# One core, three stages in one launch: the scan recurrence's softplus, shared decays and group norm rearranged, and the attention stage's norms and filter rows moved off VectorE

## The chip, the cores and the metric

The kernel runs on one NeuronCore of a Trainium2 chip. The metric is the device time of one launch in microseconds (us), lower is better. Engines are called by the names that the profile uses: PE is TensorE (matmuls), DVE is VectorE, ACT is ScalarE, POOL is GpSimd, SP is the queue that issues the DMAs.

## The reference, cut to what matters

```python
def reference(x, ...):                       # x: (4, 64, 32, 32); L = 1024 positions, 64 channels
    # 1. two selective-scan blocks (forward, backward) over the 1024 positions
    for d in ("f", "b"):
        xp, z = split(xs @ W_in)             # 128 + 128 channels
        xc = silu(conv2(xp) + conv_b)
        dt_r, Bc, Cc = split(xc @ W_x)       # 8, 16, 16
        dt = softplus(dt_r @ W_dt + b_dt)
        h = exp(dt * A[:, s]) * h + dt * xc * Bc[s]     # 16 states s, 128 channels, in sequence over t
        y = (sum_s h * Cc[s] + D * xc) * silu(z)
        out += y @ W_out
    x = silu(groupnorm(out, 4 groups)) + x
    # 2. causal attention on layer-normed tokens, one head of 64
    t = tokens(x);  t = t + attention(layernorm(t), Wq, Wk, Wv)
    # 3. four "experts" of spectral convolutions (16 filters, prefixes 1, 1/2, 1/4, 1/8 of the sequence)
    t = t + sum_i w_i * stu_i(layernorm(t)[:, :L // 2**i], sigma, phi, M_u[i], M_phi_plus[i], M_phi_minus[i])
    return from_tokens(t)
```

## The kernel before

`build` runs three stages, one after the other, with all engines meeting between them.

**Stage 1, `mamba_stage`.** The work is cut into 8 units: batch entry b (0 to 3) times direction i (forward, backward), u = 2b + i. A unit has 16 states s. For each state DVE makes a drive, `ps_d = ps_x * b_wide` (`drive_step`), and then scans it, `hidden = decay * hidden + drive` (`scan_step`, an instruction over 1024 positions). The decays are exponentials that ACT makes (`decay_of`), the products `prod = hidden * c_wide` are POOL's, and PE adds the 16 products in `ps_y` (`sum_states`). For 4 of the 16 states, `POOL_STATES`, POOL makes the drive into `drive` (`share`) and ACT writes the decay into the PSUM tile `ps_w` (`shared_decay_of`), so that DVE only scans; in the last unit this is so for one state. There are 4 `hidden`, 4 `decay` and `PAIR` = 2 `prod` buffers. While unit u is scanned, the input side of unit v = u + 1 goes through the same `ps_w` on PE and ACT: z, the convolution, the low-rank rows (`take_low`), then dt. dt is a softplus, put together by PE from four parts (`softplus_low`, `softplus_high`) and copied out by `take_dt`; DVE then makes `ps_x = dt * xc` (`dt_x`) and ACT copies it to `dtx` (`keep_dtx`). After the second scan of a unit DVE multiplies the summed `ps_y` of the unit before with its gate (`gate_of`). Each batch entry ends with a product to 64 channels (`out_product`, `norm_take`), a group norm (`norm_stats`, `norm_rstd`, `norm_scale`, `norm_silu`) and a residual sum.

**Stage 2, `attention_stage`.** A prologue and then four slots, slot b for batch entry b. In a slot PE, ACT and DVE go through 12 blocks of transposed scores, exponentials and products for b, and through the scores and row maxima of b + 1 (`reduce`, `maximum`) and the layer norm and projections of b + 2 (`center_x`, `spread_x`, `norm_x`, `normed`, `queries`, `keys`, `values`). DVE also makes the second layer norm of b - 1 (`center_x2`, `norm_x2`). `filter_rows` prepares the filters of stage 3 on DVE in slot 0, after all expert weights have been loaded; POOL weighs and sums the expert matrices (`weigh_and_sum`, `lag_matrices`, `tap_blocks`). The reciprocal roots of all norms are POOL's (`rstd`, `rstd2`).

**Stage 3, `expert_stage`.** PE convolves and mixes 16 filters for two pairs of batch entries. The diff doesn't touch it.

The order on each engine is the order in which its program is written; semaphores (`wait_ge`, `then_inc`) are the only links between engines. Every engine's program for stage 1 is a `batch` function with a loop over s, unrolled for the first and last batch entry and run as a loop for the two between.

## Time and profile before

| what | us |
|---|---|
| three timed runs | 1029.58, 1028.31, 1020.8; median 1028.31 |
| the profiled execution, its own time | 1023.59 |
| its span in the profile | 1021.8 |
| stage 1: start to first scan, scans to the last copy | 37, 508 |
| stage 2 | 161 |
| stage 3 | 315 |
| busy in the span: PE, DVE, ACT, POOL | 859.3, 768.6, 494.0, 539.1 |
| granted TensorE clock, mean, as a share of 2.4 GHz | 0.926 |

The profiled execution lies inside the range of the three runs; 1.8 us of its time lie outside the span. The stage boundaries are read from where the engines start their next program.

### The profile page before, as it was taken

To read this page: it belongs to the slowest core of one execution; us is meant where nothing else is said; L and a number is where in the kernel's file an instruction comes from. 1 tells how busy PE (TensorE), PEld (TensorE's weight loads), DVE (VectorE), ACT (ScalarE), POOL (GpSimd) and SP (SyncE) were. 2 spreads that over 40 slices of the span, in tenths; PEclk is the share of its full clock that TensorE was granted. 3 is DMA by queue.
4 is the path that set the end of the run, shared out by engine and by line. 5 is a ranking of instruction groups with operands and counts; after the bars stand their busy time and mean duration, and the time that the engine had idled before them with its cause. 6 is when DMAs were issued, how large, how long until landed. Compare 5 with 4: busy or idle time off the path is not lost. (4 is left out here: it accounts for less than half of the span.)

```text
span 1021.8 us, 10203 instructions
## 1 busy us (share of the span) xinstructions
PE 859.3 (84%) x3020; PEld 500.5 (49%) x3020; DVE 768.6 (75%) x818; ACT 494.0 (48%) x636; POOL 539.1 (53%) x364
## 2 busy tenths in 40 slices
PE   5669897986878787896676798796999999999996
PEld 2223333332333232332223455444888888888885
DVE  0698999999989999899985668565565656466664
ACT  4355464745646474563302443444455555355554
POOL 3466879786878787875644387332122222122220
PEclk9788999998999999997777989797999999999998
DMA  7667988967879788886517820000233333243332
GB/s 188 220 234 252 335 292 296 323 240 246 299 275 315 242 303 281 275 320 216 207 60 96 94 83 1 0 1 1 83 124 116 105 109 123 83 124 123 123 98 67
DMA packets 74756, 178.20 MB, mean 174 GB/s; under 512 B 23922, under 2 KB 24452, under 8 KB 74708
## 3 DMA queue, kind: packets, MB, share of 16 engines
q1 hardware_dynamic: 74724, 177.82, 54.5%
q8 instruction: 14, 0.23, 0.1%
q14 instruction: 18, 0.15, 0.1%
HBM read 175.54 MB, written 2.26 MB: 174 GB/s over the span
## 5 line engine op out<-in xcount | busy, mean ns | idle before, releaser
L424 POOL TENSOR_TENSOR prod<-hidden,c_wide 128x1024 f32<-128x1024 f32 x128 | 305.8, 2401 | 113.9 <-PE ps_y L512 75.1
L512 PE MATMUL ps_y<-prod,ident 128*128 128x512 f32 x512 | 265.5, 654 | 75.3 <-POOL prod L424 75.1
L815 DVE TENSOR_TENSOR_SCAN hidden<-decay,ps_d 128x1024 f32<-128x1024 f32 x99 | 226.4, 2287 | 13.0 <-DVE ps_d L801 1.9
L1743 PE MATMUL ps_conv<-hankel,u_high 128*128 128x512 f32 (+1 forms) x768 | 215.3, 361 | 0.0
L512 PEld LDWEIGHTS ps_y<-prod,ident 128*128 128x128 f32 x512 | 100.7, 206 | 231.0 <-POOL prod L424 118.1
L1743 PEld LDWEIGHTS ps_conv<-hankel,u_high 128*128 128x128 f32 x768 | 138.6, 189 | 25.6 <-issue 0.3
L1903 DVE TENSOR_TENSOR stack<-ps_conv,stack 64x512 fp32r<-64x512 f32 x128 | 88.3, 690 | 68.8 <-ACT stack L1866 66.4
L1743 PE MATMUL ps_conv<-hankel,u_low 128*128 128x512 f32 (+1 forms) x384 | 138.1, 360 | 0.0
L1626 POOL CAST block_mix<-even 128x256 fp32r (+1 forms) x32 | 12.7, 398 | 218.9 <-PE ps_tail L1725 218.9
L1903 DVE TENSOR_TENSOR qk<-ps_conv,qk 64x512 fp32r<-64x512 f32 x128 | 88.2, 689 | 50.0 <-ACT qk L1866 47.3
L801 DVE TENSOR_TENSOR ps_d<-ps_x,b_wide 128x1024 f32<-128x1024 f32 x99 | 121.3, 1225 | 6.1 <-ACT dtx L680 2.0
L1866 ACT ACTIVATE stack<-ps_conv 64x512 fp32r<-64x512 f32 x128 | 76.1, 594 | 82.3 <-PE ps_conv L1743 80.5
L1866 ACT ACTIVATE qk<-ps_conv 64x512 fp32r<-64x512 f32 x128 | 76.1, 594 | 62.0 <-PE ps_conv L1743 59.9
L686 ACT ACTIVATE decay<-dt_b,a_neg_b 128x1024 f32<-128x1024 f32 x51 | 57.5, 1143 | 51.5 <-DVE hidden L815 51.4
L1743 PEld LDWEIGHTS ps_conv<-hankel,u_low 128*128 128x128 f32 x384 | 72.8, 190 | 13.9
L414 POOL TENSOR_TENSOR drive<-dtx,b_wide 128x1024 f32<-128x1024 f32 x29 | 68.2, 2353 | 13.3 <-ACT dtx L680 13.3
L815 DVE TENSOR_TENSOR_SCAN hidden<-ps_w,drive 128x1024 f32<-128x1024 f32 x29 | 66.1, 2278 | 4.9 <-ACT ps_w L693 4.8
L686 ACT ACTIVATE decay<-dt_f,a_neg_f 128x1024 f32<-128x1024 f32 x48 | 54.1, 1142 | 30.8 <-DVE hidden L815 30.6
L1110 PE MATMUL ps_o<-probs,v_one 128*65 128x512 f32 (+1 forms) x96 | 45.0, 554 | 0.7 <-ACT o_t L1233 0.6
L1358 DVE TENSOR_REDUCE max_parts<-ps_s 128x1 f32<-128x512 f32 (+1 forms) x48 | 27.4, 598 | 16.8 <-PE ps_s L1068 11.9
L1228 ACT ACTIVATE probs<-ps_t 128x512 f32<-128x512 f32 (+1 forms) x48 | 24.9, 523 | 30.4 <-PE ps_o L1110 29.9
L981 POOL TENSOR_TENSOR small<-small,minus_half 128x8 f32<-128x8 f32 x4 | 6.6, 1648 | 49.3 <-DVE small L198 49.3
(293 smaller groups left out, 1179.3 us busy)
## 6 DMA issues: line engine op xcount, KB each, us to landing
b_wide<-bc_rows SPq DMA_DIRECT2D x128, 512.0 KB, 5.0
c_wide<-bc_rows SPq DMA_DIRECT2D x128, 512.0 KB, 4.7
hankel<-filters SPq DMA_DIRECT2D x32, 1026.0 KB, 5.2
plus<-in_M_phi_plus SPq DMA_DIRECT2D x2, 1024.0 KB, 11.1
minus<-in_M_phi_minus SPq DMA_DIRECT2D x2, 1024.0 KB, 16.6
x_pair<-in_x SPq DMA_DIRECT2D x2, 768.0 KB, 8.7
bc_rows<-dt_low SPq DMA_DIRECT2D x8, 128.0 KB, 4.1
out<-plus SPq DMA_DIRECT2D x4, 256.0 KB, 5.0
```

The source lines that it names most:

```text
L414: nc.gpsimd.tensor_tensor(drive[:, :], dtx[:, :], b_wide[s % BC_DEEP][:, :], ALU.mult).then_inc(share_ready, 1)
L424: nc.gpsimd.tensor_tensor(prod[k % PAIR][:, :], hidden[k % DEEP][:, :], c_wide[s % BC_DEEP][:, :], ALU.mult).then_inc(prod_ready, 1)
L512: mm = nc.tensor.matmul(out, ident[:, :], halves(prod[k % PAIR])[h], start=False, stop=(s == N - 1))
L686: nc.scalar.activation(decay[k % DEEP][:, :], dt[i][:, :], ACT.Exp, scale=a_neg[i][:, s:s + 1]).then_inc(decay_ready, 1)
L801: nc.vector.tensor_tensor(ps_d[:, :], ps_x[:, :], b_wide[s % BC_DEEP][:, :], ALU.mult).then_inc(drive_ready, 1)
L815: nc.vector.tensor_tensor_scan(hidden[k % DEEP][:, order], left[:, order], right[:, order], 0.0, ALU.mult, ALU.add).then_inc(hidden_ready, 1)
L1110: nc.tensor.matmul(ps_o[0:C + 1, lo - H * half:], v_one[b % 2][:, kt, :], probs[n % 2][:, 0:hi - lo], start=(kt == 0), stop=True, skip_gro ...
L1228: nc.scalar.activation(probs[n % 2][:, 0:hi - lo], ps_t[n % 2][:, 0:hi - lo], ACT.Exp).then_inc(probs_ready, 1)
L1358: nc.vector.tensor_reduce(max_parts[:, i, at // H:at // H + 1], ps_s[c % 2][:, 0:n], AX.X, ALU.max, negate=True).then_inc(part_ready, 1)
L1743: mm = nc.tensor.matmul(out, pairs[q][wp][:, 2 * delta + source, :], rows, start=(delta == 0 and term == 0), stop=(delta == 2 * half + 1 a ...
L1866: nc.scalar.activation(stacks[slot][0:C, source, b, :, half * 2 * HEAD:(half + 1) * 2 * HEAD], ps_conv[source][lanes(b), half, :, :], ACT. ...
L1903: nc.vector.tensor_tensor(low, ps_conv[source][lanes(b), half, :, :], high.bitcast(F32), ALU.subtract).then_inc(conv_low, 1)
```

## The change

In words, stage 1: the z projection goes ahead in the unit (PE at s = 2 in place of 4), the convolution to s = 3, the low-rank rows to 7, and the waits for the scans of the unit before are gone; the four-part sum is spread over s = 11, 12 and 13, and starts with the rectified part. The shared states are 2, 6, 9 and 15 in place of 2, 5, 9 and 15. The decays of 6 and 9 still go to `ps_w`, and DVE makes the drive of the next state ahead of these scans; those of 2 and 15 go to `ps_d`, the tile of the drives, once the scan before has read it. There are 3 decay buffers for the states that are not shared, and 4 product buffers. `dt_x` reads dt from PSUM. The first unit's softplus is summed by DVE (`first_dt`), and its drive no longer waits for `dtx`. The group norm's sums come from ACT's accumulator (`norm_take`, `norm_squares`) and go through a small DRAM tensor to be spread over the groups. Stage 2: `filter_rows` runs on POOL; `norm_x`, `norm_x2` and the square and rounding of the second norm run on ACT, the latter two norms as 8 ACTIVATEs of 64 columns; the row maximum's rounding is a reduction in place of a cast; four of seven padding memsets went to stage 1; the weights are waited for tensor by tensor.

```diff
-PAIR = 2
+PAIR = 4
+DECAYS = 3
-POOL_STATES = (2, 5, 9, 15)
+POOL_STATES = (2, 6, 9, 15)
+WIDE_SHARED = POOL_STATES[1:3]
...
+def norm_squares(nc, act, g, b, junk, data):
+    act.wait_ge(g.mixed_ready, b + 1)
+    nc.scalar.activation(junk, data, ACT.Square, scale=GN_COUNT ** -0.5,
+                         accum_out=g.sums[:, 1:2]).then_inc(g.squared_ready, 1)
+def store_sums(sp, g, b):
+    sp.wait_ge(g.squared_ready, b + 1)
+    sp.dma_start(g.rows, g.sums[:, :]).then_inc(g.rows_out, 16)
+def load_sums(sp, g, b):
+    sp.wait_ge(g.rows_out, 16 * (b + 1))
+    at_least(sp, g.step, GN_STEPS * b)
+    sp.dma_start(g.group[:, :, :], bass.AP(g.rows.tensor, 0, [[2 * GROUP, C // GROUP], [0, GROUP], [1, 2 * GROUP]])
+                 ).then_inc(g.rows_in, 16)
 def norm_stats(nc, dve, g, b):
-    dve.wait_ge(g.mixed_ready, b + 1)
-    for h in range(2):
-        chain(h + 1, nc.vector.bn_stats(g.bn[:, h, :], g.mixed[:, h * H:(h + 1) * H]))
...
-    chain(10, nc.vector.tensor_scalar(gn[:, 2:3], gn[:, 1:2], group[:, 1:2], GN_EPS, ALU.add, ALU.add))
+    dve.wait_ge(g.rows_in, 16 * (b + 1))
+    chain(1, nc.vector.tensor_reduce(gn[:, 0:2], g.group[:, :, :].rearrange("c k t -> c t k"), AX.X, ALU.add))
+    chain(2, nc.vector.tensor_scalar(gn[:, 2:3], gn[:, 0:1], gn[:, 0:1], -1.0 / GN_COUNT ** 2, ALU.mult, ALU.mult))
+    nc.vector.tensor_scalar(gn[:, 3:4], gn[:, 2:3], gn[:, 1:2], GN_EPS, ALU.add, ALU.add).then_inc(g.step, 1)
...
 # PE, stage 1
                 def gate_in(u, i, b):
-                    scanned(u - 1, POOL_STATES[0])
+                    pe.wait_ge(dtx_ready, u)
                     project(i, b, w_gate[i], z_ready)
...
+                            if s == Y_LAG:
+                                skip_in(u, i)
+                                if ahead:
+                                    conv_in(v, j, bv)
+                            if s == 4 and i == 0 and not first:
+                                pe.wait_ge(xc_ready, v + 1)
+                                out_product(b - 1)
+                            if s == 13 and ahead:
+                                add_logarithm(v, j)
...
-                                if s == 8:
+                                if s == 7:
+                                    scanned(u, WIDE_SHARED[0])
                                     low_rank(v, j)
                                 if s == 10:
-                                    scanned(u, POOL_STATES[2])
+                                    scanned(u, WIDE_SHARED[1])
                                     dt_in(v, j)
+                                if s == 11:
+                                    add_rectified(v)
                                 if s == 12:
-                                    softplus_low(v, j)
-                                if s == 13:
-                                    softplus_high(v, j)
+                                    add_exponential(v)
...
 # ACT, stage 1
                 def shared_decay_of(u, i, s, taken, count):
-                    at_least(act, taken, count)
-                    at_least(act, hidden_ready, u * N + s - 2)
-                    nc.scalar.activation(ps_w[:, :], dt[i][:, :], ACT.Exp,
+                    act.wait_ge(taken, count)
+                    nc.scalar.activation((ps_w if s in WIDE_SHARED else ps_d)[:, :], dt[i][:, :], ACT.Exp,
                                          scale=a_neg[i][:, s:s + 1]).then_inc(share_decay, 1)
...
+                            if s == 2:
+                                shared_decay_of(u, i, POOL_STATES[0], hidden_ready, u * N + POOL_STATES[0])
+                                take_z(v, j, first=first and i == 0)
...
-                            if s == 10:
-                                softplus_exp(v, j)
                             if s == 11:
+                                softplus_exp(v, j, squared=b if i == 0 else 0)
                                 softplus_ln(v, j)
                             if s == 13:
                                 take_dt(v, j)
...
-                            if s == N - 2:
+                            if s == N - 1:
+                                shared_decay_of(u, i, POOL_STATES[3], hidden_ready, u * N + POOL_STATES[3])
                                 keep_dtx(v)
+                nc.scalar.preload_act_table_set("silu_and_others")
...
 # DVE, stage 1
+                def first_dt():
+                    dve.wait_ge(exp_ready, 2)
+                    nc.vector.scalar_tensor_tensor(out=z_raw[:, :], in0=ps_w[:, :], scalar=0.0, in1=soft[:, :],
+                                                   op0=ALU.max, op1=ALU.add).then_inc(sum_step, 1)
+                    dve.wait_ge(one_plus_ready, 1)
+                    dve.wait_ge(sum_step, 1)
+                    nc.vector.scalar_tensor_tensor(out=z_raw[:, :], in0=one_plus[:, :], scalar=-1.0, in1=z_raw[:, :],
+                                                   op0=ALU.add, op1=ALU.subtract).then_inc(sum_step, 1)
+                    dve.wait_ge(ln_ready, 1)
+                    dve.wait_ge(sum_step, 2)
+                    nc.vector.tensor_tensor(dt[0][:, :], dt[0][:, :], z_raw[:, :], ALU.subtract).then_inc(dt_ready, 1)
+                    dve.wait_ge(dt_ready, 1)
+                    nc.vector.tensor_tensor(ps_x[:, :], dt[0][:, :], xc[0][:, :], ALU.mult).then_inc(dtx_ready, 1)
...
                 def dt_x(u, i):
                     dve.wait_ge(dt_ready, u + 1)
-                    at_least(dve, dtx_kept, u)
-                    nc.vector.tensor_tensor(ps_x[:, :], dt[i][:, :], xc[i][:, :], ALU.mult).then_inc(dtx_ready, 1)
+                    dve.wait_ge(dtx_kept, u)
+                    dve.wait_ge(drive_ready, driven_before(u - 1, N - 2) + 1)
+                    nc.vector.tensor_tensor(ps_x[:, :], ps_w[:, :], xc[i][:, :], ALU.mult).then_inc(dtx_ready, 1)
...
+                            if s in shared(final) and s in WIDE_SHARED:
+                                drive_step(u, s + 1, final)
+                            elif s not in shared(final) and not (s - 1 in shared(final) and s - 1 in WIDE_SHARED):
                                 drive_step(u, s, final)
...
 # stage 2: SP, POOL, ACT, DVE
+                store_sums(sp, g, B - 1)
+                load_sums(sp, g, B - 1)
                 load_expert_weights(sp, ins, e)
...
                 rstd(1)
+                filter_rows(nc, pool, e)
                 norm_rstd(nc, pool, g, a.minus_half, B - 1)
...
-                weigh_and_sum(nc, pool, e, 0, 2)
+                weigh_and_sum(nc, pool, e, 0, EXPERTS + 2)
                 rstd(2)
...
+                def norm_x(b):
+                    act.wait_ge(ln_rstd, b)
+                    for i in range(TILES):
+                        last = nc.scalar.activation(xn[:, i, :], cen[:, i, :], ACT.Copy, scale=small[:, 2, i:i + 1])
+                    last.then_inc(xn_ready, 1)
+                def norm_x2(b):
+                    act.wait_ge(ln2_rstd, b + 1)
+                    for i in range(TILES):
+                        last = nc.scalar.activation(u_all[:, i, b, :], cen2[:, i, :], ACT.Copy, scale=small2[:, 2, i:i + 1])
+                    last.then_inc(u_ready, 1)
...
-                    nc.vector.tensor_copy(neg_max[:, tiles, C], low).then_inc(max_high_ready, 1)
+                    nc.vector.tensor_reduce(neg_max[:, tiles, C], max_parts[:, tiles, 0:-(-width(2 * d) // H)], AX.X,
+                                            ALU.min).then_inc(max_high_ready, 1)
...
                         center_x2(b - 1)
-                    else:
-                        filter_rows(nc, dve, e)
```

On DVE, from the gate product of a unit to the state after the second shared scan, in the first batch entry's second unit. Before (`hidden<-ps_w,drive` is a shared scan, here of states 2 and 5; `ps_d<-ps_x,b_wide` is a drive):

```order
L796 TENSOR_TENSOR gated_f<-ps_y,gate_f 128x1024
L815 SCALAR_TENSOR_TENSOR hidden<-ps_w,drive 128x1024
L801 TENSOR_TENSOR ps_d<-ps_x,b_wide 128x1024
L815 SCALAR_TENSOR_TENSOR hidden<-decay,ps_d 128x1024
L801 TENSOR_TENSOR ps_d<-ps_x,b_wide 128x1024
L815 SCALAR_TENSOR_TENSOR hidden<-decay,ps_d 128x1024
L815 SCALAR_TENSOR_TENSOR hidden<-ps_w,drive 128x1024
L801 TENSOR_TENSOR ps_d<-ps_x,b_wide 128x1024
L815 SCALAR_TENSOR_TENSOR hidden<-decay,ps_d 128x1024
```

After:

```order
L863 TENSOR_TENSOR gated_f<-ps_y,gate_f 128x1024
L882 SCALAR_TENSOR_TENSOR hidden<-ps_d,drive 128x1024
L868 TENSOR_TENSOR ps_d<-ps_x,b_wide 128x1024
L882 SCALAR_TENSOR_TENSOR hidden<-decay,ps_d 128x1024
L868 TENSOR_TENSOR ps_d<-ps_x,b_wide 128x1024
L882 SCALAR_TENSOR_TENSOR hidden<-decay,ps_d 128x1024
L868 TENSOR_TENSOR ps_d<-ps_x,b_wide 128x1024
L882 SCALAR_TENSOR_TENSOR hidden<-decay,ps_d 128x1024
L868 TENSOR_TENSOR ps_d<-ps_x,b_wide 128x1024
L882 SCALAR_TENSOR_TENSOR hidden<-ps_w,drive 128x1024
L882 SCALAR_TENSOR_TENSOR hidden<-decay,ps_d 128x1024
```

State 2's scan now reads its decay from `ps_d`, the second shared scan is one state later, and the drive of state 7 stands ahead of it.

On ACT, the end of the same unit: the softplus of the next unit and the last shared decay. Before:

```order
L658 ACTIVATE soft<-ps_w 128x1024
L659 ACTIVATE rectified<-ps_w 128x1024
L661 ACTIVATE soft<-soft 128x1024
L686 ACTIVATE decay<-dt_b,a_neg_b 128x1024
L665 ACTIVATE one_plus<-soft 128x1024
L669 ACTIVATE dt_f<-one_plus 128x1024
L671 ACTIVATE one_plus<-one_plus 128x1024
L686 ACTIVATE decay<-dt_b,a_neg_b 128x1024
L675 ACTIVATE dt_f<-ps_w 128x1024
L693 ACTIVATE ps_w<-dt_b,a_neg_b 128x1024
L686 ACTIVATE decay<-dt_f,a_neg_f 128x1024
L680 ACTIVATE dtx<-ps_x 128x1024
```

After (`late` is the tile that held `one_plus`):

```order
L702 ACTIVATE soft<-ps_w 128x1024
L704 ACTIVATE rectified<-ps_w 128x1024
L706 ACTIVATE soft<-soft 128x1024
L711 ACTIVATE late<-soft 128x1024
L715 ACTIVATE z_raw<-late 128x1024
L718 ACTIVATE dt_f<-late 128x1024
L732 ACTIVATE decay<-dt_b,a_neg_b 128x1024
L722 ACTIVATE dt_f<-ps_w 128x1024
L732 ACTIVATE decay<-dt_f,a_neg_f 128x1024 x2
L738 ACTIVATE ps_d<-dt_b,a_neg_b 128x1024
L727 ACTIVATE dtx<-ps_x 128x1024
```

The last shared decay now stands behind both first decays of the next unit, and goes to `ps_d`.

On ACT, slot 1 of stage 2, around the place of the layer norms (`probs` are the exponentials, `xn` and `u_all` the normed tokens). Before:

```order
L1228 ACTIVATE probs<-ps_t 128x512 x2
L1221 ACTIVATE qk<-ps_m 2x256
L1228 ACTIVATE probs<-ps_t 128x512
L1221 ACTIVATE qk<-ps_m 2x256
L1241 ACTIVATE u_all<-un 128x8x64
L1228 ACTIVATE probs<-ps_t 128x256
L1199 ACTIVATE xn_t<-ps_p 64x512 x2
```

After:

```order
L1324 ACTIVATE probs<-ps_t 128x512 x2
L1317 ACTIVATE qk<-ps_m 2x256
L1276 ACTIVATE xn<-cen,small 128x64 x8
L1324 ACTIVATE probs<-ps_t 128x512
L1317 ACTIVATE qk<-ps_m 2x256
L1324 ACTIVATE probs<-ps_t 128x256
L1286 ACTIVATE u_all<-cen,small 128x64 x8
L1289 ACTIVATE u_high<-u_all 128x8x64
L1295 ACTIVATE xn_t<-ps_p 64x512 x2
L1324 ACTIVATE probs<-ps_t 128x256
```

The two groups of eight and `u_high` are new on ACT and stand between exponentials, in place of one copy.

## Rows read from the trace of the kernel before

**Rows 1.** Busy time by stretch: core, stretch, length, busy of each engine, PEclk, DMA.
```profile
37.00:545.40 508.40, 404.01 (x836) 159.18 (x836) 469.74 (x310) 253.27 (x238) 380.32 (x164) 0.91 0.75 259
545.40:706.50 161.10, 127.21 (x536) 72.46 (x536) 107.64 (x225) 62.10 (x107) 79.75 (x49) 0.87 0.30 44
```

**Rows 2.** Groups of DVE's instructions, by shape, 60 to 525 us: busy, mean, idle before.
```profile
L815 DVE TENSOR_TENSOR_SCAN hidden<-decay,ps_d 128x1024 f32<-128x1024 f32 x94 | 215.0, 2287 | 12.4 <-DVE ps_d L801 1.9
L801 DVE TENSOR_TENSOR ps_d<-ps_x,b_wide 128x1024 f32<-128x1024 f32 x94 | 115.1, 1225 | 4.0 <-DVE gn L151 0.7
L815 DVE TENSOR_TENSOR_SCAN hidden<-ps_w,drive 128x1024 f32<-128x1024 f32 x28 | 63.8, 2279 | 4.9 <-ACT ps_w L693 4.8
L789 DVE TENSOR_TENSOR ps_x<-dt_b,xc_b 128x1024 f32<-128x1024 f32 x4 | 8.2, 2061 | 3.1 <-ACT dt_b L675 3.1
...
L145 DVE TENSOR_SCALAR group_w<-group_t 64x32 f32<-64x32 f32 x3 | 5.5, 1818 | 0.1
L796 DVE TENSOR_TENSOR gated_f<-ps_y,gate_f 128x1024 f32<-128x1024 f32 x4 | 4.9, 1218 | 0.7 <-PE ps_y L512 0.6
```

**Rows 3.** DVE in order of time: the products that end a unit (units 0, 1, 2, 6).
```profile
95.90 1.38 DVE L789 TENSOR_TENSOR ps_x<-dt_b,xc_b 128x1024 f32<-128x1024 f32 x1 [3.09 <-ACT dt_b L675]
...
152.12 1.26 DVE L789 TENSOR_TENSOR ps_x<-dt_f,xc_f 128x1024 f32<-128x1024 f32 x1
...
207.28 3.25 DVE L789 TENSOR_TENSOR ps_x<-dt_b,xc_b 128x1024 f32<-128x1024 f32 x1
...
450.09 1.92 DVE L789 TENSOR_TENSOR ps_x<-dt_b,xc_b 128x1024 f32<-128x1024 f32 x1
```

**Rows 4.** Order of time at the start: first table load, dt's copy, first drive.
```profile
10.63 1.28 ACT L631 ACT_TABLE_LOAD   x1 [10.63 <-PE ps_w L452]
...
31.45 1.02 ACT L675 ACTIVATE dt_f<-ps_w 128x1024 f32<-128x1024 f32 x1 [6.95 <-PE ps_w L486]
...
35.70 1.23 DVE L801 TENSOR_TENSOR ps_d<-ps_x,b_wide 128x1024 f32<-128x1024 f32 x1 [1.96 <-ACT dtx L680]
```

**Rows 5.** DVE in order of time: a group norm's first instruction and the drive behind it.
```profile
223.52 1.38 DVE L135 BATCH_NORM_STATS2 bn<-mixed 64x6 f32<-64x512 f32 x2
...
230.94 1.23 DVE L801 TENSOR_TENSOR ps_d<-ps_x,b_wide 128x1024 f32<-128x1024 f32 x1 [0.19 <-DVE gn L151]
```

**Rows 6.** ACT in order of time: two decays, a copy of 1024 columns, an exponential of 256.
```profile
251.61 2.19 ACT L686 ACTIVATE decay<-dt_b,a_neg_b 128x1024 f32<-128x1024 f32 x2
...
257.56 1.02 ACT L659 ACTIVATE rectified<-ps_w 128x1024 f32<-128x1024 f32 x1
...
573.74 0.39 ACT L1228 ACTIVATE probs<-ps_t 128x256 f32<-128x256 f32 x1 [0.81 <-PE ps_o L1110]
```

**Rows 7.** PE in order of time: sums of 128x1024, at either clock.
```profile
60.87 3.75 PE L452 MATMUL ps_w<-x_pair,w_conv_b 128*128 128x512 f32 x4 [6.12 <-DVE hidden L815]
...
263.11 1.88 PE L486 MATMUL ps_w<-rectified,ident 128*128 128x512 f32 x4
264.82 1.88 PE L512 MATMUL ps_y<-prod,ident 128*128 128x512 f32 x4
```

**Rows 8.** Groups of DVE's instructions, by shape, in stage 2 (527 to 720 us).
```profile
L1372 DVE CAST neg_max<-lowest 128x2 fp32r<-128x2 f32 x8 | 6.7, 834 | 0.3
L1536 DVE TENSOR_TENSOR even<-even 16x512 fp32r<-16x512 f32 x2 | 5.0, 2490 | 0.1
L1317 DVE TENSOR_TENSOR cen<-cen,small 128x512 f32<-128x512 f32 x3 | 4.8, 1599 | 0.0
...
L1535 DVE CAST even<-even 16x512 fp32r<-16x512 f32 x2 | 2.4, 1206 | 0.0
```

**Rows 9.** PE's waits in stage 2, the longest.
```profile
PE ps_s L1063 <- DVE max_parts L1358: 16.1, 8, 7.7
```

**Rows 10.** Busy time of slots 0 and 1 of stage 2, columns as in rows 1.
```profile
568.00:608.70 40.70, 34.47 (x141) 19.57 (x141) 25.35 (x41) 14.81 (x27) 24.03 (x12) 0.87 0.48 88
608.70:652.50 43.80, 34.17 (x142) 19.38 (x143) 31.75 (x55) 16.07 (x29) 31.22 (x14) 0.84 0.00 0
```

377 lines of the change are left out of this document (202 added, 175 removed).

## The prediction

> **What bounds the kernel now.** I read the busy time by stretch first, to split the span. Stage 1's scans take 508.4 us with DVE busy for 469.7, so DVE sets their pace; stage 2 takes 161.1 us with PE busy for 127.2 and DVE for 107.6, a ping-pong [rows 1]. Stage 3, 315 us, is untouched and stays. Then DVE's groups, for what makes up its time. A scan takes 2.29 us and a drive 1.23 us; 94 + 28 scans and 94 drives are 394 of the 465 us of that view [rows 2]. The end products of the units, in order of time, give the floor of a unit: unit 2 lasts from 152.12 to 207.28 us, 55.2 us [rows 3], and by rows it holds 12 x (2.29 + 1.23) + 4 x 2.28 + 1.22 + 1.26 = 53.8 us of work; the rest is the tenth of a us between dependent instructions. So a unit can't be shorter than about 55.2 us unless it has less DVE work, and the change leaves scans and drives as many as they were (12 and 4 in a unit, 15 and 1 in the last).
>
> **Stage 1, units 1 to 6.** From 95.90 to 450.09 us six units take 354.2 us [rows 3], 23.0 over six floors. Part of it is group norm: its statistics keep DVE from 223.52 to 230.94 us, 7.4 us [rows 5], and of this the tiny L145 has 1.8 us on average, far above the 0.2 us that its size would suggest [rows 2]. Part is the product that ends a unit: 2.06 us on average, up to 3.25 us [rows 2, 3], against 1.22 us for the gate product, which has one input in PSUM [rows 2]. The rest is waits, the shared decay's 4.9 us first. The change makes the end product read PSUM, so 1.22 us. The norm's ten instructions become three of about 0.2 us, plus three as before for the scale, 1.4 us for each batch entry (0.75 with hops for the statistics, 0.65 for the scale). Its sums are made by ACT and spread by two small DMAs, which SP issues at its s = 9 and 11 while DVE is some states behind; a scan step or two lies between load and use, so I count their flight at nothing; were it exposed, it would be up to one such step, 3.7 us, for each of three norms.
>
> New waits on DVE: the decays of states 2 and 15 can be written only when the scan before has ended. That is ACT's 1.1 us [rows 6] plus two semaphore hops, against a gate product or end product of 1.22 us that DVE does meanwhile: 0.1 us exposed if ACT is free. At state 15 ACT isn't always. I follow the chain from the end of scan 10, on which decay 13's buffer now waits: one decay 1.1, two copies 2.0, then on PE five groups (rectified, a sum of products, exponential, and the two last parts) at a pitch of 1.72 us [rows 7], 8.8 with the tail, dt's copy 1.0, two decays 2.15, the shared decay 1.1 [rows 6], some 0.5 of hops: 16.6 us. DVE needs for scans 11 to 14 and the end product 4 x 3.66 + 1.3 = 15.9 us. So 0.7 us of wait in a unit, less where a norm stands in between; I take 0.5. Six units then give 6 x 0.5 + 3 x 0.75 + 2 x 0.65 = 6.5 over the floor, against 23.0: a gain of 16.5, of which I keep 15 for stretches at PE's lower clock.
>
> POOL's extra slack (4 product buffers) I count at nothing: DVE's waits in rows 2 name it nowhere. POOL is busy for 380 of 508 us [rows 1] and gets no more work in this stage.
>
> **Stage 1, start.** Before, ACT runs out of work at 31.45 - 6.95 = 24.50 us, after the logarithm and one copy; the first drive is at 35.70 [rows 4]. Now DVE subtracts and multiplies, 2 x 1.23 and hops, 2.7 us, after the logarithm, which ended one copy (1.0) earlier; this replaces 35.7 - 23.5 = 12.2 us. The table load of 1.28 us [rows 4] leaves the path, and so do the gate's activation and the rectified copy, 1.0 each [rows 6]. All told 12.8 us. Against it: two of the four new DVE instructions read SBUF only, while POOL works on a small power; the same kind of product took 3.25 in place of 1.26 us beside POOL [rows 3], so up to 2 us each. Bounds 6 (with PE at its lower clock as well) and 12.8; I take 10, nearer the upper row since POOL's work there is one short instruction. Unit 0 loses a 3.1 us wait for dt [rows 3] but has nothing to cover the decay of state 2 (1.3): a gain of 1.
>
> **Stage 1, last unit.** The norm's statistics leave it, and its scale stays: 7.4 less 0.75 by rows 5, 5 if L145 had taken 0.2; I take 6. The attention work in it is the same. Four product buffers spare about 1 us at the very end. Stage 1 in all: 15 + 10 + 1 + 6 + 1 = 33 us.
>
> **Stage 2.** Prologue: PE no longer waits for the padding, but the chain norm, transposes, PE scores, row maxima, group norm scale and silu is as long as before, since the eight ACTIVATEs of `norm_x` take about 8 x 0.25 = 2 us, for one DVE instruction of 512 columns: nothing gained. (By rows 6, 768 columns cost 1.02 - 0.39 us, so 64 columns take 0.23; a scale from SBUF adds 0.12, as a decay's 1.14 against the copy's 1.02 shows; overlap takes off 0.1.) Slot 0: `filter_rows` leaves DVE. Its two subtractions are 5.0 us and its two casts 2.4, 7.4 together [rows 8]. Behind it PE waits: 16.1 us in 8 waits for row maxima, the longest 7.7 [rows 9]. DVE would next wait for the tokens' copy, so 5.5 of 7.4 are gained, and 1 more from a PE that isn't left idle. Slot 1: DVE instructions that read SBUF only are stretched beside POOL's matrix sums: `cen` has 1.60 us on average for 512 columns [rows 8], where a drive of 1024 takes 1.23 [rows 2], and casts of two columns have 0.83 [rows 8]. They leave DVE or, as reductions, can't be held up. The longest wait of PE stands right there. PE is busy for 34.2 of slot 1's 43.8 us, and for 34.5 of slot 0's 40.7 [rows 10], so 34 is the floor of either: at most 6.5 and 9.6. I take 5.5 and 8.5, for POOL now does the filter rows and six matrices ahead of `rstd(2)`, and ACT waits for it in order, ahead of an exponential that PE needs: 1 to 2 us.
>
> Slots 2 and 3: DVE has less, ACT has 2.0 + 0.6 us more between two exponentials: I take +1 in slot 3 and nothing in slot 2. The tail, last token product to stage 3, becomes a chain over DVE, ACT, POOL and ACT again: two more hops, and 2.0 us of ACT for half a drive's columns on DVE: +2. Stage 2: 5.5 + 8.5 - 1 - 2 = 11, with bounds of 4 and 17.
>
> On one price the Trainium skill can be asked. Its page "ScalarE: Activation LUTs", section "Rules for kernel authors", says to multiply on VectorE and not on ScalarE, and the section "What ACT_TABLE_LOAD costs" gives 280 ns and 0.833 ns for each column with a pointer operand, 93 ns of it overlapped. By that page eight such ACTIVATEs are an estimated 1.9 us, so the sum would be the same within 0.2 us; the rule speaks against the move, and would be right here if DVE had no other work.
>
> **The sum.** 33 + 11 = 44 us off the profiled execution's 1023.6 us: 979.6. The median of the three runs lies 4.7 above that execution, the lowest run 2.8 below, so I put the changed median at 981.
>
> **The rivals.** (1) *The decays in `ps_d` are not covered.* If ACT reaches states 2 and 15 late, DVE waits for a whole ACTIVATE and hops, 1.3 us, and for what stands ahead of it, 1.1 more at state 15: some 2.4 + 1.3 = 3.7 us in each of 7 units, 26 less the 3.5 counted: about 1003. For it: ACT's queue is in order, and my chain has no slack. Against: ACT is busy for half of the time only [rows 1].
>
> (2) *PE falls to its lower clock inside the dt chain.* A group of four matmuls takes 3.75 us at 1.2 GHz, after a wait of 6.12 us, and 1.88 at 2.4 GHz [rows 7]. Five groups would add 8.6 us to a chain without slack, in all seven units 60 us: 1041, slower than before. It decides from about five units of seven (44/8.6 = 5.1). For it: the change makes PE wait for scan 6, scan 9 and the rectified copy. Against: these waits come out at 2 to 2.5 us by my durations, the granted clock was 0.91 in the scans [rows 1], and PE is busy for 404 of the 508 us, so it is seldom left idle for long.
>
> The Trainium skill's page "TensorE: Matmul & The Clock Gate", section "HAM oscillation", tells of a kernel whose every pause for data started it again at the low clock; by such a mechanism (2) would come out.
>
> (3) *Stage 2 gives nothing*, because ACT in order waits for POOL's roots and holds the exponentials: 992.
>
> (4) *The change doesn't shorten DVE's norm and end products*, as they were waits for something else counted as busy: 13 less, 994.
>
> (5) *More is gained*, with both slots at PE's floor and no chain wait: 968.
>
> **How the numbers follow.** Forecast (972 to 988) 0.50; (1) 0.13; (2) 0.04; (3) 0.09; (4) 0.07; (5) 0.12; something that I haven't seen, of either sign, 0.05. The range takes in the forecast, (3), (4) and (5) whole and stops short of (1) and (2): 964 to 1000. Less than 1% is about what a measurement of this kernel can't tell from no change. Faster by over 1%: all but (2) and part of the unseen, 0.93; same 0.03; slower 0.04.
>
> **What would show it.** First scan at about 27 us; unit lengths of 55 to 57 us; end product at 1.2 us, L145's place empty; DVE's wait for `ps_d`'s decay under 1 us a time; slots 0 and 1 of about 35 us each; stage 3 unchanged at 315. Units of 60 us and more with PEclk near 0.5 in them would mean (2); waits of 1 to 2.5 us on the shared scans (1). A DMA chain of the norm's sums that comes in late, or PE waiting on ACT for `xn`, would make the forecast wrong without any of these.

## The result, and the profile after

Four runs of the changed kernel gave 984.49, 981.74, 977.89 and 983.11 us, median 982.42; four of the kernel before gave a median of 1024.57. The ratio is 0.958, with a 95% interval of 0.952 to 0.964: about 42 us less. The time came out 1.4 us above the forecast of 981. That closeness is partly luck: by the two profiled executions 39.2 us were gained where the sum had 44, and the experiments below show errors of opposite sign in stage 1, which cancel for the most part.

The first rows of the changed kernel are its windows, one for each of units 1 to 6 from end product to end product, and behind the dots the stretches of stage 2: ahead of slot 0, slots 0, 1 and 2, and slot 3 with the tail. Columns as in [rows 1].

```profile
86.60:143.20 56.60, 46.44 (x99) 18.32 (x98) 53.31 (x32) 30.70 (x30) 46.73 (x20) 0.94 0.84 300
143.20:201.20 58.00, 51.32 (x109) 20.05 (x108) 53.77 (x34) 34.12 (x34) 47.10 (x21) 0.94 0.81 291
201.20:259.00 57.80, 47.65 (x104) 19.25 (x103) 53.75 (x34) 34.42 (x33) 49.09 (x22) 0.97 0.86 289
259.00:315.50 56.50, 50.52 (x111) 20.26 (x110) 53.62 (x34) 34.65 (x35) 46.70 (x21) 0.97 0.85 306
315.50:371.40 55.90, 45.60 (x100) 18.30 (x99) 53.67 (x34) 32.50 (x31) 49.04 (x22) 0.97 0.90 298
371.40:428.00 56.60, 50.59 (x111) 20.19 (x110) 53.61 (x34) 34.93 (x36) 46.94 (x22) 0.97 0.82 301
...
515.70:541.30 25.60, 16.89 (x64) 10.67 (x64) 13.21 (x37) 13.63 (x25) 15.49 (x14) 0.73 0.93 103
541.30:576.40 35.10, 33.35 (x141) 18.94 (x142) 16.39 (x36) 16.68 (x36) 33.74 (x17) 0.90 0.74 123
576.40:609.90 33.50, 30.70 (x145) 17.76 (x146) 18.65 (x50) 20.14 (x47) 17.98 (x9) 1.00 0.00 1
609.90:636.90 27.00, 25.34 (x123) 15.11 (x123) 16.83 (x48) 14.23 (x33) 8.06 (x10) 1.00 0.00 1
636.90:667.60 30.70, 16.35 (x68) 7.82 (x67) 10.75 (x32) 15.09 (x37) 3.38 (x5) 0.84 0.00 0
```

Against the marks of before the two profiled executions (spans of 1021.8 and 982.6 us) divide as follows; a mark is the start of the instruction named, and a minus is time gained.

| stretch | before | after | difference | forecast |
|---|---|---|---|---|
| start to the first scan | 37.04 | 28.13 | -8.9 | -10 |
| first scan to the end product of unit 0 | 58.86 | 58.43 | -0.4 | -1 |
| units 1 to 6 | 354.19 | 341.47 | -12.7 | -15 |
| last unit, to the end of its last scan | 79.47 | 73.90 | -5.6 | -6 |
| to the copy of `mixed` | 14.61 | 13.75 | -0.9 | -1 |
| ahead of slot 0 | 23.92 | 25.58 | +1.7 | 0 |
| slot 0 | 40.68 | 35.12 | -5.6 | -5.5 |
| slot 1 | 43.74 | 33.51 | -10.2 | -8.5 |
| slot 2 | 28.08 | 26.96 | -1.1 | 0 |
| slot 3 to the copy of its last output | 16.07 | 19.11 | +3.0 | +1 |
| tail | 9.93 | 11.60 | +1.7 | +2 |
| stage 3 | 315.2 | 315.0 | -0.2 | 0 |

The first mark is the least certain: in kernels that don't differ up to there it lay between 25.2 and 28.1 us. The units vary too: three kernels further below have this same stage 1 and change stage 2 alone, and their profiles have 337.2, 342.9 and 339.3 us for units 1 to 6, where this one has 341.5. So a difference of under some 6 us in that row, between two single profiles, isn't told from scatter.

Next, the same kernel's groups of DVE's and POOL's instructions in the scans (30 to 515 us): busy time, mean of one in ns, and the idle time ahead of them.

```profile
L882 DVE TENSOR_TENSOR_SCAN hidden<-ps_w,drive 128x1024 f32<-128x1024 f32 x15 | 34.2, 2279 | 0.0
L882 DVE TENSOR_TENSOR_SCAN hidden<-ps_d,drive 128x1024 f32<-128x1024 f32 x14 | 32.1, 2290 | 9.3 <-ACT ps_d L738 5.4 <-issue 3.2
L856 DVE TENSOR_TENSOR ps_x<-ps_w,xc_b 128x1024 f32<-128x1024 f32 x4 | 4.8, 1212 | 0.3 <-ACT dt_b L722 0.3
...
L451 POOL TENSOR_TENSOR prod<-hidden,c_wide 128x1024 f32<-128x1024 f32 x128 | 300.8, 2356 | 99.0 <-DVE hidden L882 93.4 <-PE ps_y L546 3.1 <-DMA c_wide<-bc_rows 1.2
```

The end product has 1.21 us ([rows 2] had 2.06), and the scans of states 6 and 9 (`ps_w`) wait for nothing. But before the scans of states 2 and 15 (`ps_d`) DVE stands idle for 9.3 us, 7.4 of them at state 15. And POOL's products now wait for DVE's scans. In the kernel before they waited for PE's sums; its group of the same products (60 to 525 us):

```profile
L424 POOL TENSOR_TENSOR prod<-hidden,c_wide 128x1024 f32<-128x1024 f32 x122 | 291.7, 2404 | 104.5 <-PE ps_y L512 68.5 <-DVE hidden L815 35.6
```

That POOL waited for PE's sums is the sign whose meaning I had missed.

Here is unit 1's state 15 in order of time, ACT, DVE and PE:

```profile
131.06 3.75 PE L515 MATMUL ps_w<-rectified,ident 128*128 128x512 f32 x4 [0.86 <-ACT rectified L704]
134.60 2.31 PE L546 MATMUL ps_y<-prod,ident 128*128 128x512 f32 x4
136.75 1.88 PE L515 MATMUL ps_w<-soft,ident 128*128 128x512 f32 x4
...
142.10 1.02 ACT L722 ACTIVATE dt_f<-ps_w 128x1024 f32<-128x1024 f32 x1 [6.08 <-PE ps_w L515]
143.15 2.19 ACT L732 ACTIVATE decay<-dt_f,a_neg_f 128x1024 f32<-128x1024 f32 x2
143.15 1.23 DVE L856 TENSOR_TENSOR ps_x<-ps_w,xc_f 128x1024 f32<-128x1024 f32 x1 [0.70 <-ACT dt_f L722]
145.25 1.10 ACT L738 ACTIVATE ps_d<-dt_b,a_neg_b 128x1024 f32<-128x1024 f32 x1
146.43 2.29 DVE L882 TENSOR_TENSOR_SCAN hidden<-ps_d,drive 128x1024 f32<-128x1024 f32 x1 [2.05 <-ACT ps_d L738]
```

ACT copies dt, then writes two decays of the next unit (2.19 us) and only then the decay that DVE wants now; DVE waits 2.05 us. The first row is a group of PE at 3.75 us, the duration of the lower clock (1.2 GHz) in [rows 7], after 0.86 us without work; the granted clock in it is 0.50. Units 1 and 2 have one such group each, the other five have 1.95 to 2.27 us for it, and these two have the long waits, 2.05 and 2.12 us, against 0.25 to 1.03.

### The profile page after: what moved, and what is told of

It reads as the page before. It is cut to its first block and busy times, and to the rows that moved or that the text cites. A ratio compares the mean times of both kernels' runs of the same rounds, so it can differ in the third digit from the quotient of the medians.

```text
span 982.6 us, 10220 instructions
## 1 busy us (share of the span) xinstructions
PE 841.4 (86%) x3004; PEld 493.4 (50%) x3004; DVE 722.8 (74%) x774; ACT 511.6 (52%) x706; POOL 534.3 (54%) x366
## 5 line engine op out<-in xcount | busy, mean ns | idle before, releaser
L451 POOL TENSOR_TENSOR prod<-hidden,c_wide 128x1024 f32<-128x1024 f32 x128 | 300.8, 2356 | 99.0 <-DVE hidden L882 93.4
L546 PE MATMUL ps_y<-prod,ident 128*128 128x512 f32 x512 | 247.3, 627 | 42.8 <-POOL prod L451 42.7
L546 PEld LDWEIGHTS ps_y<-prod,ident 128*128 128x128 f32 x512 | 98.2, 198 | 185.7 <-issue 117.1
L1733 POOL CAST block_mix<-even 128x256 fp32r (+1 forms) x32 | 12.7, 398 | 218.9 <-PE ps_tail L1832 218.9
L732 ACT ACTIVATE decay<-dt_f,a_neg_f 128x1024 f32<-128x1024 f32 x48 | 54.2, 1142 | 38.4 <-DVE hidden L882 37.1
L1460 DVE TENSOR_REDUCE max_parts<-ps_s 128x1 f32<-128x512 f32 (+1 forms) x48 | 27.5, 598 | 27.1 <-PE ps_s L1144 13.4
L882 DVE TENSOR_TENSOR_SCAN hidden<-ps_d,drive 128x1024 f32<-128x1024 f32 x14 | 32.1, 2290 | 9.3 <-ACT ps_d L738 5.4
L882 DVE TENSOR_TENSOR_SCAN hidden<-ps_w,drive 128x1024 f32<-128x1024 f32 x15 | 34.2, 2279 | 0.0
```

The costliest lines, as they stand in the source:

```text
L451: nc.gpsimd.tensor_tensor(prod[k % PAIR][:, :], hidden[k % DEEP][:, :], c_wide[s % BC_DEEP][:, :], ALU.mult).then_inc(prod_ready, 1)
L546: mm = nc.tensor.matmul(out, ident[:, :], halves(prod[k % PAIR])[h], start=False, stop=(k % N == N - 1))
L732: nc.scalar.activation(decay[decay_slot(s, last)][:, :], dt[i][:, :], ACT.Exp, scale=a_neg[i][:, s:s + 1]).then_inc(decay_ready, 1)
L882: nc.vector.tensor_tensor_scan(hidden[k % DEEP][:, order], left[:, order], right[:, order], 0.0, ALU.mult, ALU.add).then_inc(hidden_ready, 1)
L1460: nc.vector.tensor_reduce(max_parts[:, i, at // H:at // H + 1], ps_s[c % 2][:, 0:n], AX.X, ALU.max, negate=True).then_inc(part_ready, 1)
```

## The experiments

All times are medians of four or five runs. They were taken in three groups, each on another chip, and the kernel before gave 1023.8, 1025.1 and 1022.9 us beside them. The changed kernel itself was run only with the first result (982.42 us, from 977.9 to 984.5, where the kernel before gave 1024.6), so differences of 1 to 3 us from it can't be told from none. Each experiment is an edit of the changed kernel unless the text says otherwise.

**State 15's decay first.** ACT writes the decay of state 15 straight behind its copy of dt, two steps of its loop earlier, and copies `dtx` one step earlier.

```diff
                             if s == 13:
                                 take_dt(v, j)
-                            if s == N - 1:
                                 shared_decay_of(u, i, POOL_STATES[3], ...)
+                            if s == 14:
                                 keep_dtx(v)
```

> The changed kernel with one thing moved: ACT writes the decay of state 15 into ps_d straight after it has copied dt, ahead of the next unit's first two decays, and copies dtx between those two. Theory A: DVE's waits for that decay, 0.67, 2.05, 2.12, 0.95, 0.30, 1.03 and 0.25 us (7.4 in seven units), come from the two decays of 2.19 us that stand ahead of it in ACT's queue; they fall to under 0.3 us each, and 5 to 7 us are gained: 976 to 978 us against 982.4. Rival B: the wait is set by the chain over PE (rectified, exponential, logarithm, dt) alone; then the waits move to the end product and under 1 us is gained. Rival C: the next unit's first scan or its dtx comes late in their place, and nothing is gained.

975.16 us (974.38 to 977.46), 7.3 less; ratio to the kernel before 0.953 (0.951 to 0.955). Units 1 to 6 take 334.7 us, 55.8 each, below all four profiles with the old order (337.2 to 342.9). The rows, for the end of unit 1:

```profile
135.23 1.02 ACT L722 ACTIVATE dt_f<-ps_w 128x1024 f32<-128x1024 f32 x1 [3.89 <-PE ps_w L515]
...
137.68 1.21 DVE L856 TENSOR_TENSOR ps_x<-ps_w,xc_f 128x1024 f32<-128x1024 f32 x1
137.80 1.12 ACT L738 ACTIVATE ps_d<-dt_b,a_neg_b 128x1024 f32<-128x1024 f32 x1 [1.55 <-DVE hidden L882]
...
138.86 1.13 ACT L732 ACTIVATE decay<-dt_f,a_neg_f 128x1024 f32<-128x1024 f32 x1
139.01 2.29 DVE L882 TENSOR_TENSOR_SCAN hidden<-ps_d,drive 128x1024 f32<-128x1024 f32 x1
```

The decay is now written while DVE makes the end product, and the scan behind it starts without a wait. Theory A holds; the waits at state 15 fall from 7.4 us in seven units to 0.6. 55.8 us is close to the 55.2 that the prediction called the floor.

**Two product buffers.**

```diff
-PAIR = 4
+PAIR = 2
```

> The changed kernel with two product buffers in place of four. Theory A (the prediction's): nothing, within 1 us, except about 1 us at the very end of stage 1, since DVE never waits for POOL in the scans; POOL's products wait for PE's sums instead of for DVE. Rival B: POOL falls back against DVE (its products, 2.35 us, and the shared drives leave little slack), the hidden buffers fill, and DVE waits: 5 to 15 us slower, with waits of the scans for prod in the trace.

1008.90 us (1005.58 to 1012.22): 26.5 us slower, for buffers that the prediction counted at nothing. Of this 23 us lie in stage 1, 16.7 in units 1 to 6 (358.2 us; the kernel before needed 354.2). Rival B's direction was right; its size was too small, and the waits name POOL's drive and not its products. First the groups of DVE and POOL (30 to 515 us), then the end of unit 5 in order of time:

```profile
L882 DVE TENSOR_TENSOR_SCAN hidden<-ps_w,drive 128x1024 f32<-128x1024 f32 x15 | 34.2, 2281 | 5.6 <-POOL drive L441 5.6
L882 DVE TENSOR_TENSOR_SCAN hidden<-ps_d,drive 128x1024 f32<-128x1024 f32 x14 | 32.1, 2290 | 22.5 <-POOL drive L441 20.5 <-ACT ps_d L738 1.2
...
L451 POOL TENSOR_TENSOR prod<-hidden,c_wide 128x1024 f32<-128x1024 f32 x126 | 294.7, 2354 | 117.4 <-PE ps_y L546 91.6 <-DVE hidden L882 25.8
```

```profile
381.10 1.88 PE L515 MATMUL ps_w<-dt_f,ident 128*128 128x512 f32 x4
382.81 3.60 PE L546 MATMUL ps_y<-prod,ident 128*128 128x512 f32 x8
...
384.84 2.36 POOL L451 TENSOR_TENSOR prod<-hidden,c_wide 128x1024 f32<-128x1024 f32 x1 [4.48 <-PE ps_y L546]
387.16 2.34 POOL L441 TENSOR_TENSOR drive<-dtx,b_wide 128x1024 f32<-128x1024 f32 x1
...
389.63 2.29 DVE L882 TENSOR_TENSOR_SCAN hidden<-ps_d,drive 128x1024 f32<-128x1024 f32 x1 [2.92 <-POOL drive L441]
```

In the second piece PE does three groups for dt in a row (the last at 381.10) before it sums products at 382.81. POOL, whose both buffers are full, waits 4.48 us. In its queue behind that product stands the drive for state 15, which is made at 387.16, and DVE waits 2.92 us for it. In the kernel before, PE's program has the sum of a step ahead of its dt groups; the change puts the sum of state 13's step behind the last two dt groups, and with it behind their wait for ACT's logarithm.

Another 3.3 us of the 26.5 lie in slot 0 of stage 2, which takes 38.4 us in this profile against 35.1. There POOL waits 2.73 us for a transfer of expert weights, its `rstd(2)` is late, ACT waits 3.56 us for that ahead of `norm_x`, and PE 3.83 us for ACT. It isn't shown that the buffers bring this about.

**The same with that drive made earlier.**

```diff
-PAIR = 4
+PAIR = 2
...
+                            if s == 11 and not (last and i == 1):
+                                share(u, POOL_STATES[3])
-                            if s + SHARE_AHEAD in shared(last and i == 1):
+                            if s != 12 and s + SHARE_AHEAD in shared(last and i == 1):
                                 share(u, s + SHARE_AHEAD)
```

> The changed kernel with two product buffers, as in the experiment of 1009 us, and POOL's drive for state 15 made one state earlier: behind the product of state 11 and not of state 12. Theory A: two buffers hurt mainly because POOL, held for a free product buffer while PE works on dt, starts that drive late, and DVE waits for it (20.5 us in seven units); made earlier it is in time, and 12 to 20 us come back: 989 to 997 us. Rival B: POOL's backlog moves on to DVE in another way (a full ring of hidden buffers, the next unit's dtx or first shared drive), and under 5 us come back: 1004 us or more.

987.98 us (984.77 to 991.92): 21 of the 26.5 us come back, the top of Theory A. The scans of `ps_d` wait 6.7 us in place of 22.5, and POOL's products still wait 82.2 us for PE. What stays are 5.6 us of waits for the drive of state 6, as many as with two buffers alone; slot 0 has 34.4 us here. So the fault of two buffers is mainly not that POOL waits; it is what stands behind the waiting instruction in its queue.

**The kernel before with four product buffers.**

```diff
-PAIR = 2
+PAIR = 4
+DECAYS = 3
...
-        one_plus = sb("one_plus", [D, L])
+        one_plus = a.late[:, 0:L]
```

> The kernel before with four product buffers in place of two, and what gives them room: three decay buffers in place of four (dealt out over the states that have one), and the buffer of 1 + exp shared with the attention's first tokens; nothing else of the change. Two product buffers in the changed kernel gave 1009 us, 27 slower than four. Theory A: the buffers by themselves are worth that much, since POOL's products wait for PE's sums in the kernel before as well (75 us): 1000 us or less against 1024. Rival B: they only mend what the rest of the change breaks (PE's sums stand behind its dt groups, the shared drive of state 15 comes late): within 4 us of 1024. Rival C: part of each, 1008 to 1018, by products on DVE that meet POOL less often.

1017.51 us (1016.74 to 1018.15), ratio 0.993 (0.991 to 0.995): 7.6 us. Rival C. The run changes product and decay buffers together and doesn't tell them apart. Two rows of its DVE (60 to 525 us) matter:

```profile
L805 DVE TENSOR_TENSOR ps_x<-dt_b,xc_b 128x1024 f32<-128x1024 f32 x4 | 4.8, 1208 | 0.0
L831 DVE TENSOR_TENSOR_SCAN hidden<-ps_w,drive 128x1024 f32<-128x1024 f32 x27 | 61.5, 2278 | 10.2 <-ACT ps_w L709 10.2
```

The end product has 1.21 us here although it reads dt from SBUF, as in [rows 2], where it had 2.06. And the gain is partly eaten, since DVE now waits 10.2 us for the shared decay where it waited 4.9 [rows 2]: in units 1 to 6 DVE is busy for 6.3 us less, and they are 1.2 us shorter (353.0).

**The end product from SBUF again.**

```diff
-                    nc.vector.tensor_tensor(ps_x[:, :], ps_w[:, :], xc[i][:, :], ...)
+                    nc.vector.tensor_tensor(ps_x[:, :], dt[i][:, :], xc[i][:, :], ...)
```

> The changed kernel with the end product of a unit reading dt from SBUF, as before, in place of PSUM. Theory A (the price is in the operand): an instruction with both inputs in SBUF is stretched while POOL works, the end product goes from 1.21 us back to about 2.1 on average (up to 3.25), 5 to 6 us of DVE in seven units; as state 15's decay comes late anyway, 2 to 6 us of it show. Rival B (the fourth rival of the prediction): its length was a wait counted as busy, for something that the change has removed elsewhere; it stays at 1.2 us and nothing changes.

983.23 us (982.43 to 985.28), no difference that can be told; units 1 to 6 take 343.4 us, 1.9 more, which is inside the scatter. Six of the seven products take 1.21 to 1.37 us and one 3.89. Neither theory has it: the length doesn't follow from the operands alone, and it is no hidden wait for something that the change removed. Two of the seven products, each with POOL beside it:

```profile
257.78 1.21 DVE L856 TENSOR_TENSOR ps_x<-dt_f,xc_f 128x1024 f32<-128x1024 f32 x1
257.95 3.26 POOL L451 TENSOR_TENSOR prod<-hidden,c_wide 128x1024 f32<-128x1024 f32 x1 [0.18 <-DVE hidden L882]
...
312.46 4.66 POOL L451 TENSOR_TENSOR prod<-hidden,c_wide 128x1024 f32<-128x1024 f32 x2
314.33 3.89 DVE L856 TENSOR_TENSOR ps_x<-dt_b,xc_b 128x1024 f32<-128x1024 f32 x1
```

At 257.78 DVE starts first and takes 1.21 us, and it is POOL's product, 0.17 us later, that is stretched, to 3.26 from 2.35. At 314.33 POOL is already at work, with two products back to back (4.66 us to 317.12), and DVE's product takes 3.89. With both inputs in SBUF, who comes second waits for the other. With four buffers POOL is never far behind: it starts on a product when DVE ends a scan, so at an end product it starts with DVE or a little later and mostly comes second. The Trainium skill's page "SBUF — State Buffer", section "Terms", says of the port pair of the two engines that it is exclusive and held for a whole instruction; these rows agree, and add that a waiting DVE can lose to POOL's next instruction as well.

**The norm's statistics on DVE again**, with `bn_stats` and eight small instructions, where the change has its three.

```diff
-                         accum_out=g.sums[:, 1:2]).then_inc(g.squared_ready, 1)
+        chain(h + 1, nc.vector.bn_stats(g.bn[:, h, :], g.mixed[:, h * H:(h + 1) * H]))
...
-                            if s == 9:
-                                store_sums(sp, g, u // 2 - 1)
-                            if s == 11:
-                                load_sums(sp, g, u // 2 - 1)
```

> The changed kernel with the group norm's statistics made by DVE as before (two bn_stats and eight small instructions), at the places where the change has its three, without the two DMAs and ACT's squares. Theory A (the terms of the sum): 6.6 us more of DVE for each of three batch entries in the scans, some 20 us, and 0 to 5 in the fourth, which lies in stage 2: 1003 to 1008 us. Rival B: only the work by size counts (two bn_stats of 0.6 us and eight of 0.2), the rest of the 7.4 us before was waiting that had to be somewhere: 2.5 us each, 990 us.

984.92 us (981.08 to 987.62), 2.5 more, which can't be told from none. In units 1 to 6 DVE is busy for 8.7 us more, 2.9 for each norm, and they take 5.1 us more (the busy time doesn't scatter: it is 325.2 or 325.3 us in all four profiles of the same stage 1). The waits of the `ps_d` scans fall from 9.3 to 5.1 us: in the three units with a norm ACT catches up meanwhile (0.12 us each), and only one group of PE in this profile has the lower clock, where the changed kernel's had two. Theory A's 20 us are ruled out; Rival B's mechanism fits, at a third of the 7.6 us that its 990 stood for. A norm in order of time:

```profile
186.65 1.38 DVE L138 BATCH_NORM_STATS2 bn<-mixed 64x6 f32<-64x512 f32 x2
186.81 2.36 POOL L442 TENSOR_TENSOR prod<-hidden,c_wide 128x1024 f32<-128x1024 f32 x1 [1.17 <-DVE hidden L869]
...
188.43 0.77 DVE L142 SCALAR_TENSOR_TENSOR stats<-stats 64x1 f32<-64x1 f32 x1
...
189.68 0.17 DVE L148 TENSOR_SCALAR group_w<-group_t 64x32 f32<-64x32 f32 x1
...
190.78 1.23 DVE L855 TENSOR_TENSOR ps_d<-ps_x,b_wide 128x1024 f32<-128x1024 f32 x1 [0.22 <-DVE gn L154]
```

The whole takes 4.1 us. The norm of [rows 5] took 7.4, but it was the longest of three: the other two of the kernel before took 5.1 and 6.2. POOL's product runs from 186.81 to 189.17, and the small instruction at 188.43 ends at 189.20, with it. L148, which is the L145 of [rows 2], comes when POOL has nothing to do, as DVE isn't scanning: 0.17 us, against 1.82. In the kernel before with four buffers, where the statistics stand behind scan 2 and meet one of POOL's shared drives, it still has 1.84 us in the median. So for this instruction it is the place that matters, and for the end product the buffers or, as the next experiment shows, its operand.

**Two buffers and both old steps.** The edits of the last two experiments and `PAIR = 2`.

> The changed kernel with two product buffers, the norm's statistics on DVE and the end product's dt from SBUF, all three at once. With four buffers the two old steps cost 3 us of DVE for each norm (5 us in the units) and 1.9 us, against 7.4 and up to 3.25 us each in the kernel before. Theory A: the price of a DVE instruction that reads SBUF only is what is left of the POOL instruction that it meets; with two buffers POOL is behind and always busy, so the norm's ten instructions take 6 us and more again, the end products 2 us on average, and the time is 1022 to 1034 us, 13 to 25 over the 1009 of two buffers alone. Rival B: the prices are those of four buffers and add up: 1011 to 1016 us. Rival C: DVE waits for POOL's drive there anyway, and the old steps hide in that wait: 1009 to 1011.

1014.47 us (1012.53 to 1016.73), 5.6 over two buffers alone. The end products are long again, as a backlog of POOL would have it. The first two rows are this run's; the third and fourth are those of two buffers alone, where the product reads dt from PSUM:

```profile
L843 DVE TENSOR_TENSOR ps_x<-dt_f,xc_f 128x1024 f32<-128x1024 f32 x3 | 8.8, 2944 | 0.0
L843 DVE TENSOR_TENSOR ps_x<-dt_b,xc_b 128x1024 f32<-128x1024 f32 x4 | 7.9, 1974 | 0.0
...
L856 DVE TENSOR_TENSOR ps_x<-ps_w,xc_b 128x1024 f32<-128x1024 f32 x4 | 4.8, 1208 | 0.0
L856 DVE TENSOR_TENSOR ps_x<-ps_w,xc_f 128x1024 f32<-128x1024 f32 x3 | 3.6, 1207 | 0.0
```

So the operand matters as well. With two buffers and dt from PSUM the product took 1.21 us in all seven units, though a product of POOL's was running when DVE began in six of them, and began with it in the seventh (in unit 5 DVE began at 385.51, and POOL's ran from 384.84, see above). With two buffers and dt from SBUF it took 1.64 to 3.27 us. Either edit, four buffers or PSUM, is enough for 1.21 us.

The norm's small instructions stay short (0.7 and 0.17 us for the two that were long), by their place. Units 1 to 6 get 15.6 us longer (373.8 us), but the way from `mixed` to the start of slot 1 is 5.8 us shorter than with two buffers alone (56.5 against 62.2). Nearly all of that is slot 0, 32.8 against 38.4 us: POOL's wait for the weights and those of ACT and PE behind it are not there this time. The start, unit 0 and the last unit are 1.5 us shorter each; why is open. The total is Rival B's, the rows show Theory A's price for one of the two parts: as a sum inconclusive.

**Filter rows on DVE again** (slot 0, where they stood before).

```diff
-                filter_rows(nc, pool, e)
...
                     if b:
                         center_x2(b - 1)
+                    else:
+                        filter_rows(nc, dve, e)
```

> The changed kernel with filter_rows back on DVE, in slot 0 where it stood before. Theory A (the prediction's): slot 0 of stage 2 goes from 35.1 us back to about 40.7, as 7.4 us of DVE stand ahead of row maxima that PE waits for: 987 to 988 us. Rival B: it is POOL's part that counts: POOL starts its matrix sums only behind DVE's rows as before, DVE's SBUF instructions of slot 1 meet them there, and slot 1 becomes longer as well: 990 us or more. Rival C: 2 us or less, the slot's time before came from elsewhere.

988.57 us (982.27 to 991.52), 6.2 more. Slot 0 has 41.1 us in its profile, slot 1 its 33.5 unchanged. The time alone lies between Theory A's 988 and Rival B's 990; the unchanged slot 1 speaks for Theory A, with 5.5 us forecast for slot 0 and 6.0 found.

**Layer norms' products on DVE again.**

```diff
-                        if after and n == 7:
-                            norm_x(b + 2)
-                        if b and n == 9:
-                            norm_x2(b - 1)
...
+                    if after:
+                        norm_x(b + 2)
                     if ahead:
                         reduce(b + 1, 4, 8)
                         maximum(b + 1, 2)
+                    if b:
+                        norm_x2(b - 1)
+                        split_u(b - 1)
```

> The changed kernel with the products of both layer norms (and the cast of the second) back on DVE, where they stood before; filter rows, reductions and the order of the sums on POOL stay as changed. Theory A (the prediction's): slot 1 goes from 33.5 to 40 us or more, since these instructions read SBUF only and are stretched by POOL's matrix sums; slot 3 and the tail get back 2 to 4 us that ACT's eight pieces cost: about 986. Rival B: stretching was worth little once the filter rows had left, and ACT's pieces cost as much as they spare: 979 to 982, no slower.

991.65 us (985.86 to 997.65), 9.2 more; the profiled execution is the slowest of the four, so its slots (39.6, 42.5, 32.2 us, and 27.3 from there to stage 3) overstate. Theory A's mechanism holds in slot 1, and its 986 us were too low: it had no price for slots 0 and 2, which grow from 35.1 and 27.0 us. Rows of DVE in slot 1 (578 to 621 us):

```profile
L1422 DVE TENSOR_TENSOR xn<-cen,small 128x512 f32<-128x512 f32 x1 | 2.8, 2827 | 1.0 <-POOL small L1051 1.0
...
L1427 DVE TENSOR_TENSOR u_all<-cen,small 128x512 f32<-128x512 f32 x1 | 1.9, 1912 | 0.0
```

512 columns take 1.9 to 2.8 us beside POOL's matrix sums; on ACT each of these steps of eight pieces takes 2.0 us. Slot 3 and the tail are 3.4 us shorter than in the changed kernel, which is what ACT's pieces cost there.

**Both on DVE**: stage 1 as changed, the attention much as before.

> The changed kernel with both filter rows and the layer norms' products back on DVE where they stood before: stage 1 as changed, the attention much as before. Apart, the rows gave 988.6 us and the norms 991.7, against 982.4. Theory A: they add, in slot 0 (the rows) and slots 1 and 2 (the norms): 995 to 1001 us, and stage 1's part of the change is about 26 of 42 us. Rival B: they share a wait (POOL's matrix sums start later, so they meet the norms' products in other places): 990 to 994.

995.79 us (989.20 to 997.64), 13.4 more than the changed kernel, where the two alone gave 6.2 and 9.2: they add, less 2 us (Theory A). So of some 41 us 13 belong to these two moves, and 27 (1022.88 less 995.79) to the rest. That rest is stage 1 by the profiles: stage 2 takes 162.8 us here and 162.4 in the kernel before.

**A better version.** State 15's decay first, and in stage 2, in ACT's queue:

```diff
-                        if b and n == 2:
-                            keep_x2(b - 1)
                         if b and n == 3:
-                            square2(b - 1)
+                            keep_x2(b - 1)
...
+                        if b and n == 5:
+                            square2(b - 1)
...
-                        if b and n == 9:
+                        if b and ahead and n == 9:
                             norm_x2(b - 1)
...
                 take_output(B - 1, 1)
+                norm_x2(B - 2)
                 keep_x2(B - 1)
                 square2(B - 1)
```

and the last norm's product on DVE.

> The changed kernel with three moves. First the order of ACT at state 15 as in the experiment before (975.2 us). Then in stage 2 the copy of a finished batch entry to x2 one block later and the squares of its norm two blocks later in ACT's queue, since ACT waits there for DVE (0.63 + 2.14 us in slots 1 and 2, 1.57 in slot 3) ahead of an exponential that PE needs. Then the norm of entry 2 behind the last copy of an output instead of ahead of it (2.65 us of ACT in slot 3), and the last norm's product on DVE in one instruction of 0.7 us instead of eight of 2.0. Theory: 1 us in each of slots 1 and 2, 3 to 4 us in slot 3 with the tail: 969 to 971 us. Rival: DVE's or POOL's own order holds these slots (the row maxima, the next norm's chain), and 974 to 975 remains.

968.38 us (966.47 to 969.88), ratio 0.944 (0.942 to 0.947): 14 us below the changed kernel and 56 below the one before. Its stage 2, with windows as above from slot 1 on:

```profile
567.30:599.50 32.20, 30.69 (x145) 17.79 (x146) 18.71 (x50) 20.20 (x47) 20.04 (x10) 1.00 0.00 1
599.50:625.20 25.70, 25.10 (x122) 15.06 (x123) 16.77 (x47) 14.15 (x32) 8.07 (x10) 1.00 0.00 1
625.20:651.70 26.50, 16.34 (x68) 7.84 (x68) 11.40 (x33) 13.15 (x30) 3.37 (x4) 0.84 0.00 0
```

Slots 1 and 2 are 1.3 us shorter each, slot 3 with the tail 4.2: a little more than forecast.

**And its first norm on DVE.**

```diff
-                norm_x(1)
...
+                nc.vector.tensor_tensor(xn[:, :, :], cen[:, :, :], small[:, 2, :]..., ALU.mult)
```

> The best kernel so far (968.4 us) with one more step: the product of the attention's first layer norm, ahead of slot 0, on DVE in one instruction (0.7 us) in place of ACT's eight (2.0 us). Theory A: the chain norm, transposes, queries, slot 0 is shortened by 1.2 us: 967. Rival B: DVE's instruction reads SBUF only and meets POOL's filter rows (0.63 and 1.35 us each), and its row maxima stand behind it: 968 to 970, nothing gained.

969.39 us (966.03 to 971.34): nothing gained, Rival B. The product begins while POOL works on the filter rows and takes 1.72 us, where the same size took 0.68 in the kernel before:

```profile
520.98 1.35 POOL L1646 TENSOR_TENSOR even<-even 16x512 fp32r<-16x512 f32 x1
521.15 1.72 DVE L1548 TENSOR_TENSOR xn<-cen,small 128x512 f32<-128x512 f32 x1
```

It stands behind row maxima on DVE and ends at 522.88, where ACT's eight ran from 520.32 to 522.34 in the profile of the better version.

## Why the prediction was right, and where it wasn't

- **Stage 1's bound.** DVE's floor of 55.2 us for a unit stands: 55.8 us once the waits are gone, and 55.6 in the better version.
- **The step that failed: "POOL's extra slack (4 product buffers) I count at nothing: DVE's waits in rows 2 name it nowhere."** They are worth 26.5 us in the changed kernel and, with what gives them room, 7.6 in the one before. The waits of before told of the old order of PE's queue. The change moves PE's last dt groups, with their wait for ACT, ahead of a sum, and I followed what that does to dt and to the clock (rival 2), not to the queue behind it: PE's sum, POOL's product, POOL's drive, DVE's scan. With two buffers DVE waits 20.5 us for that drive and 5.6 for that of state 6; with four, no wait before a scan names POOL.
- **The terms for the end product and the norm (together 16.5 us in units 1 to 6, as what lies over the floor)** were priced with durations of a DVE that met a POOL with a backlog, and the norm's 7.4 us were those of the longest of three. With two buffers both together do cost 15.6 us in the units. With four they add, put back one at a time, 2.6 and 8.7 us to DVE's busy time there, 1.9 and 5.1 us to the units and nothing clear to the launch. The end product's 2.06 us fall to 1.21 by the buffers without PSUM, and by PSUM without the buffers; so that term isn't the operand's alone. Rival 4 (waits counted as busy) names half of it, for that busy time was a wait for POOL.
- **The units' gain of 15** came out as 12.7. With product buffers, norm and end product all as before, the six units of the changed kernel take 373.8 us, 19.6 more than in the kernel before. So the rest of the change (PE's order, the shared decays in `ps_d`, three decay buffers) costs 19.6 us by itself, norm and end product give back 15.6, and the buffers 16.7 on top of that. How the 19.6 us are shared out within the rest stays open: ACT's order at state 15 and the place of POOL's drive were moved one at a time, PE's order and the decay buffers were not.
- **State 15's wait**, 0.5 us a unit: 7.4 us in seven, 1.05 each, up to 2.12. I had its chain (16.6 against 15.9 us) and the low clock in it, but had put the decays of the next unit ahead of the shared one as unavoidable. Their order was free: 7.3 us. Rival 1's wait for ACT is there in small, at state 15 only. Rival 2's mechanism is seen in two units, in one of five groups, 1.9 us each and not 8.6. Of the waits that it gives PE, that for scan 9 was there before; only that for scan 6 and the place of the rectified copy are new.
- **Start**, 10: 8.9. The instructions that read SBUF only, three and not two of the four, took 1.23 us each and no more: POOL's power had ended at 22.64 us, and the first of them began at 22.94. The first scan came at 28.13 and not at 27.
- **Last unit**, 6: 5.6. **Very end**, 1: 0.9.
- **Slot 0**, 5.5: 5.6, and 6.0 when undone. **Slot 1**, 8.5: 10.2. ACT's wait for POOL's `rstd(2)`, for which 1 to 2 us were taken off, isn't in this profile; it is in slot 0 with two buffers (3.56 us) and with the end product from SBUF (2.02 us), where POOL had waited for the expert weights. **Slot 3**, +1: +3.0, since ACT waits 1.57 us for DVE's tokens in `keep_x2`, one block earlier than before, which wasn't costed, and then does 2.65 us of the norm ahead of the last output, which was costed at 1. **Tail**, +2: +1.7. **Ahead of slot 0**, 0: +1.7; the same eight ACTIVATEs on the path that I took as equal to one DVE instruction (2.02 against 0.7 us). Put back on DVE it gained nothing: in that place it met POOL's filter rows and took 1.72 us.
- **Rivals 3 and 5**: stage 2 gave 10.5 us, not nothing; the floor of slot 1 (34) was reached.

## What to carry to other kernels

A wait table says what holds an engine in the order that the program has now. When a change puts new work ahead of something in an in-order queue, follow that queue on to the engine that it feeds, and to whatever stands behind the waiting instruction there; slack that nobody used before can be what the new order lives on. And a duration that comes from two engines at one port is a property of how they meet and of where the operands lie, not of the instruction alone: undo one step at a time, and two together, before believing in its price.

## What the runs showed of the hardware that I had not expected

- A DVE product of 1024 columns with both inputs in SBUF took 1.21 or 3.89 us in one kernel, by whether POOL's product started after it or was running with another one behind it; with an input in PSUM it took 1.21 to 1.23 in all seven places, also with two buffers, where POOL's product was running when it began in six of seven. The loss goes the other way too: POOL's product took 3.26 in place of 2.35 us.
- Small DVE instructions suffer the same: one of 64 partitions x 32 columns took 1.84 us or 0.17, by its place.
- Two groups of four matmuls fell to 1.2 GHz after waits of only 0.86 and 0.76 us, while waits of 1.52 and 1.58 us in other units left the clock at 2.4 GHz. Three kernels with the same stage 1 had one, three and one such group in their profiles; no run here tells what decides it.
